# Eight-core attention and quantized-FFN layer: stage barriers replaced by single waits, one LayerNorm loop reordered, attention accumulators reassigned

## What is computed

```
x = hidden_states                        # 16 x 2048 x 1024 f32, two sequences a core
q, k, v = LN(x) @ wq + bq, LN(x) @ wk, LN(x) @ wv + bv   # 16 heads of 64
q, k = rope(q, k)                        # on the last 1024 positions
a = softmax(q k^T / 8) v
x = x + LN(a @ wo + bo)
h = bit_linear(LN(x), w1)                # 1024 -> 4096; activations to 8 bits per token,
h = silu(depthwise_conv1d(h, taps=3))    # weights to -1, 0, 1 times one scale
x = x + LN(bit_linear(h, w2))            # 4096 -> 1024
```

## Time and profile before

| | us |
|---|---|
| median of 11 runs | 4889.68 |
| lowest and highest run | 4879.98, 4936.07 |
| the profiled execution: its time | 4886.25 |
| its span on core 5, the slowest | 4884.7 |
| spans of the eight cores | 4842.8 to 4884.7 |
| busy on core 5: PE, DVE, ACT, POOL | 2952.0, 2054.0, 1861.9, 51.7 |
| mean granted TensorE clock, core 5 | 0.836 |

### The profile page before, as it was taken

The page is one execution under the profiler, slowest core; times in us unless marked ns, Lnnn a source line. Parts: engine busy times, 40 slices in busy tenths (PEclk is TensorE's granted clock), DMA queues, the critical chain, the costliest instruction groups (busy, mean ns, idle before and its releaser), DMA issues. The chain is left out here.

```text
span 4884.7 us, 42219 instructions; the slowest of 8 cores (4842.8 to 4884.7 us)
## 1 busy us (share of the span) xinstructions
PE 2952.0 (60%) x12366; PEld 1063.9 (22%) x12366; DVE 2054.0 (42%) x3536; ACT 1861.9 (38%) x2155; POOL 51.7 (1%) x94
## 2 busy tenths in 40 slices
PE   0000587888884231787888882235885887277677
PEld 0000232211211111331122220112332333133233
DVE  1333332544454444343445545443443444333433
ACT  0113236766772211337677771211221222333322
POOL 0000000000000000000000000000000000100000
PEclk9999998878876665898788886667997998588798
DMA  7776100000000222100000001223111111423231
GB/s 194 259 258 213 52 27 1 3 3 5 3 3 22 67 76 78 37 20 0 3 5 3 3 5 41 67 67 121 50 51 56 48 48 44 142 93 115 87 121 65
DMA packets 154953, 311.69 MB, mean 64 GB/s; under 512 B 65445, under 2 KB 98277, under 8 KB 150630
## 3 DMA queue, kind: packets, MB, share of 16 engines
q1 hardware_dynamic: 139946, 235.54, 14.8%
q0 software_dynamic: 14784, 73.44, 4.5%
HBM read 206.16 MB, written 98.60 MB: 62 GB/s over the span
## 5 line engine op out<-in xcount | busy, mean ns | idle before, releaser
L701 ACT ACTIVATE ptil<-sc,negM 128x1024 bf16<-128x1024 f32 x1024 | 1060.1, 1142 | 389.8 <-PE sc L640 388.9
L637 PE MATMUL sc<-qres,kres 64*128 64x512 bf16 x1024 | 431.7, 422 | 45.6 <-ACT ptil L701 4.5
L640 PE MATMUL sc<-qres,kres 64*128 64x512 bf16 x1024 | 441.7, 432 | 0.0
L711 PE MATMUL accA<-ptil,vres 128*65 128x512 bf16 x768 | 348.8, 454 | 38.2 <-DVE attA L730 37.2
L715 PE MATMUL accA<-ptil,vres 128*65 128x512 bf16 x768 | 320.8, 418 | 75.9 <-DVE attA L730 75.9
L1186 PE MATMUL p2a<-w2q,ring 128*128 128x512 bf16 x1024 | 239.9, 398 | 181.1 <-DVE outt L1203 156.0
L1012 ACT ACTIVATE hsb<-pcA,convb_s 128x512 bf16<-128x512 f32 x128 | 88.2, 689 | 525.8 <-PE pcA L1003 493.4
L875 PE MATMUL pw<-ident,xqtm 128*128 128x128 bf16 x256 | 32.4, 306 | 417.5 <-DVE xqtm L866 417.5
L979 PE MATMUL pwA<-xqd,w1q 128*128 128x512 bf16 x1024 | 245.1, 382 | 44.9 <-DVE hsc L988 44.9
L159 ACT ACTIVATE stat<-stat 128x1 f32<-128x1 f32 x128 | 25.6, 200 | 576.6 <-DVE stat L154 576.6
L979 PE MATMUL pwB<-xqd,w1q 128*128 128x512 bf16 x1024 | 243.3, 381 | 0.0
(11 more groups left out here) (208 smaller groups left out, 4524.5 us busy)
## 6 DMA issues: line engine op xcount, KB each, us to landing
hs_sp<-hsb SPq DMA_DIRECT2D x64, 512.0 KB, 2.6
ring<-hs_sp SPq DMA_DIRECT2D x8, 4096.0 KB, 15.3
wstg<-w1t SPq DMA_DIRECT2D x8, 2048.0 KB, 11.2
wstg<-w1t POOLq DMA_DIRECT2D x8, 2048.0 KB, 13.7
wstg<-w2t SPq DMA_DIRECT2D x8, 2048.0 KB, 11.8
wstg<-w2t POOLq DMA_DIRECT2D x8, 2048.0 KB, 13.1
xra<-x SPq DMA_DIRECT2D x32, 512.0 KB, 3.8
xrb<-x SPq DMA_DIRECT2D x32, 512.0 KB, 4.6
```

What stands on the lines that cost most here:

```text
L637: TE.matmul(sc[sl][:, 0:512], kc_[0:64, kt * 128:(kt + 1) * 128], qc_[0:64, qc * 512:(qc + 1) * 512], start=True, stop=True, tile_position ...
L640: smmv[g] = st.inc(TE.matmul(sc[sl][:, 512:1024], kc_[64:128, kt * 128:(kt + 1) * 128], qc_[64:128, qc * 512:(qc + 1) * 512], start=True, ...
L701: expv[pl] = ss.inc(S.activation(ptil[pl][:], sc[sl][:], AF.Exp, bias=negM[:, p:p + 1], scale=1.0))
L711: TE.matmul(accAd[:], dc4[:, kt, 0:65], ptil[pl][:, 0:512], start=(kt == 0), stop=(kt == NKT - 1))
```

## The change

- All barriers between stages go, except the first one at the start, the one ahead of the w1 stage and the last. In their place stand waits of single engines on the semaphores above, in front of the next stage or inside it.
- In LN1 each tile calls `ln_chain`, which is `ln_stats` and `ln_fin` one after the other; the statistics of the next tile are no longer issued ahead.
- In attention head A alternates between `accA` and `accA2`, and head B always uses `accB`. The A matmul of a block waits for the copies of A two blocks back (`epivA`), the B matmul for the B copy of the block before (`epivB`, the second of the four copies). The order of the four copies stays.

```
-        bar()                                    # weights -> LN1
+        sv.wait(TE); ss.wait(TE); sv.wait(V)
...
-                    ln1_stats(0)
                     for i in range(NT128):
-                        if i + 1 < NT128:
-                            ln1_stats(i + 1)
-                        r_ap, mb_ap, mbv_ = ln_fin((i % 4) * 4, stats_v[i])
+                        dxr[i % 3].wait(V, xload[i])
+                        r_ap, mb_ap, mbv_ = ln_chain(xr[i % 3][:], (i % 4) * 4)
...
-                bar()                            # LN1 -> QKV
+                sv.wait(TE)
+                ss.wait(TE)
...
+                    for qeng in (SY, G):         # ahead of the first load of wsb
+                        dstg[0].wait(qeng)
+                        dstg[1].wait(qeng)
+                        st.wait(qeng)
+                        if s == 0:
+                            dss[0].wait(qeng)
+                            dss[1].wait(qeng)
+                            dsq[0].wait(qeng)
+                            dsq[1].wait(qeng)
+                            sv.wait(qeng)
+                            ss.wait(qeng)
...
-                bar()                            # QKV -> attention
+                    sv.wait(TE)
+                    ss.wait(TE)
...
-                        accAd = accr[(2 * qc) % 3]
-                        accBd = accr[(2 * qc + 1) % 3]
+                        accAd = accA if qc % 2 == 0 else accA2
                         if kt == 0:
-                            sv.wait(TE, epivN[(2 * qc) % 3])
+                            sv.wait(TE, epivA[qc % 2])
                         TE.matmul(accAd[:], ...)
                         if kt == 0:
-                            sv.wait(TE, epivN[(2 * qc + 1) % 3])
+                            sv.wait(TE, epivB)
-                            accBd[:], dc4[:, kt, 65:130], ptil[pl][:, 512:1024],
+                            accB[:], dc4[:, kt, 65:130], ptil[pl][:, 512:1024],
...
+                    dtb[0].wait(TE)
+                    dtb[1].wait(TE)
                     dtb[0].wait(SY)
                     dtb[1].wait(SY)
-                bar()                            # attention -> Wo
+                    sv.wait(TE)
+                    ss.wait(TE)
...
-                bar()                            # Wo -> LN1 of the next sequence
+                st.wait(V)
+                sv.wait(TE)
+                ss.wait(TE)
...
-        bar()                                    # w1 stage -> w2 stage
+            sv.wait(TE)
+            ss.wait(TE)
...
+            drl.wait(G)
+            st.wait(G)
+            dhs.wait(S)
+            dhs.wait(V)
+            dsw.wait(S)
+            dsw.wait(V)
             for c in range(HC):
                 drl.inc(G.dma_start(w2q[:, c * H:(c + 1) * H], w2qt_sp[c]), 16)
...
                     drl.wait(G)
+                    dsw.wait(G)
```

More of the change, by code:

```diff
@@ L348, in build_nc @@
                 s_.wait(SY)
-        bar()
+        sv.wait(TE)
+        ss.wait(TE)
+        sv.wait(V)
         _ph = ExitStack()
@@ L611, in build_nc @@
                     sc = [sc0, sc1]
-                    accr = [accA, accA2, accB]
                     expv = [0, 0, 0]
@@ L615, in build_nc @@
                     epiv = 0
-                    epivN = [0, 0, 0]
+                    epivA = [0, 0]
+                    epivB = 0
                     bcv = 0
@@ L723, in build_nc @@
                             V.tensor_copy(lbufB[0:1, qc * 512:(qc + 1) * 512],
-                                          accBd[64:65, :])
-                            epivN[(2 * qc + 1) % 3] = sv.inc(V.tensor_copy(
+                                          accB[64:65, :])
+                            epivB = sv.inc(V.tensor_copy(
                                 tmpB[p % 2][:, qc * 512:(qc + 1) * 512],
-                                accBd[0:64, :]))
+                                accB[0:64, :]))
                             V.tensor_copy(lbufA[0:1, qc * 512:(qc + 1) * 512],
                                           accAd[64:65, :])
-                            epivN[(2 * qc) % 3] = epiv = sv.inc(V.tensor_copy(
+                            epivA[qc % 2] = epiv = sv.inc(V.tensor_copy(
                                 attA[0:64, p * T + qc * 512:p * T + (qc + 1) * 512],
```

## The result

The change made the kernel faster: ratio 0.959 of the kernel before, 95% interval 0.9557 to 0.9622. On the median of 4889.68 us that is 4689 us, 4673 to 4705 by the interval. The forecast was 4715 us, a ratio of 0.9643, and its range began at 4700, 11 us above what was measured. The direction and the mechanism were right; sizes of single terms were not, the step-36 term and the range's low end above all, and the last part says by how much. The median over all 12 runs is 4703.08 us; four of them had one die at a lower clock, and the ratio leaves such runs out.

What follows compares the result with a forecast made beforehand. ScalarE was taken to set attention's pace where not stopped, mostly by waits for scores; -87.4 - 59.8 - 19.5 - 14.8 + 15.4 - 5.3 = -171.4 from 4886.25 gave 4715 us, range 4700 to 4812.

Steps and rivals of the forecast that it cites:

- the step-36 term: Attention, where the reciprocals are spread: ten waits of 13.16 us take the short form of 11.68, -14.8 us.
- the range's low end: 4700 us: the forecast less 15 for the barriers' far end, LN1's low end and step 36 in its shortest form.
- The LN1 term: LN1 loop: statistics no longer issued ahead expose the square root's round trip, 0.48 us for each of 32 tiles, +15.4 us.
- The border wait: Attention block borders: B's matmul starts earlier, ScalarE's wait falls from 2.04 to 0.63 us at 62 borders, -87.4 us.
- The clock: Attention behind borders: with a TensorE gap of about 0.9 us the clock stays up and 115 slow steps go, -59.8 us.
- the excess of the border waits: Attention borders: waits longer than 2.04 us because their matmuls ran slow lose the excess, -19.5 us.
- Barriers: Between stages: single waits save -5.3 us together, between 0 and -9; -2.9 of it from w2q's earlier load before w2.
- The slowest core: Whole kernel: core 5, last already at the start of attention, stays the slowest.
- No slow spell stayed behind a border: Answers the rival for attention borders that the slow spells all stay: 4809 us, chance 0.10.
- VectorE was not late: Answers the rival that reciprocals hold up B's copy at 28 attention borders: 4993 us, chance 0.04.
- the release that doesn't come: Rival for attention borders: B's matmul still starts only after all four copies, 4896 us, chance 0.06.

Runs made afterwards that it cites:

- the kernel with three copies: Head B's first matmul of a block waits for three copies, not two, against the changed kernel; ratio 0.9788, attention 727.0 and 732.9 us.

## Why the prediction was right, and where it failed

The step that failed is the term for step 36, -14.8 us, together with the low end of the range built on it: measured, the waits at step 36 fell by 24.2 us, and the slow steps behind them, which the sum had at no change, by some 3 more. The LN1 term erred the other way, and the rest of the miss lies in which core is slowest.

- *The border wait.* Right: 1.41 us less at 62 borders; TensorE's gap "about 0.9 us" is 0.93, ScalarE's wait 0.63 is 0.63.
- *The clock.* Right as to whether, and near as to size: the slow steps behind borders cost 57.8 us (forecast 59.8), the excess of the border waits fell by 17.1 (forecast 19.5). The nearest row, QKV's clean gaps of 1.14 us, was the right one to go by, since the new gap of 0.93 us is shorter still. It would not have served for a longer one: at 1.65 us slow steps come, as the kernel with three copies shows. The rule of the Trainium skill (TensorE: Matmul & The Clock Gate, section "A second HAM failure mode: psum-queue depth-cycling") is told without gap lengths; here it holds at 1.65 and 2.35 us and not at 0.93 us, though PSUM buffers are cycled in all three.
- *Step 36: the term that failed in attention.* The prediction put it that step 36 "takes the short form (11.68)", 14.8 us in all. Shorter forms than any row of before had were there. Granted clock in a step 36 of the changed kernel, its first half and then from the fall on:

```profile
887.10:893.40 6.30, 4.27 (x18) 0.92 (x16) 2.05 (x4) 3.22 (x3) 0.00 (x0) 1.00 0.00 1
893.42:903.66 10.24, 7.36 (x18) 1.33 (x18) 5.65 (x8) 2.23 (x2) 0.00 (x0) 0.50 0.00 0
```

  and TensorE's rounds in it:

```profile
891.94 0.61 PE L670 MATMUL pib<-invrA,ones1f 1*64 1x512 f32 x1 [1.65 <-DVE invbB L680]
894.66 1.08 PE L670 MATMUL pib<-invrA,ones1f 1*64 1x512 f32 x1 [1.64 <-DVE invbB L680]
898.27 1.08 PE L670 MATMUL pib<-invrA,ones1f 1*64 1x512 f32 x1 [1.64 <-DVE invbB L680]
```

  The clock falls only after the second round: the rounds are 2.72 us apart at full clock and 3.61 at half. The 14 waits at step 36 sum to 153.9 us, 24.2 less than the 178.1 before and not 14.8, and 37 slow steps follow them (two of 1.81 us among them) instead of 43, another 3 us. The step of the earlier trace rows came right behind a slow spell: the clock was at 0.50 just before it and again from within its second round on, so that its rounds start 2.72, 3.07 and 3.61 us apart, where here they start 2.72, 2.72 and 3.61 apart. It was a row of the disturbed kernel, and I took it for the undisturbed value. That the clock falls at all inside step 36 is not the border's doing: it does so in the changed kernel too, on all eight cores, and not when the pauses are filled.
- *The low end of the range.* It takes 15 us off the forecast for three ends, but the prediction's own figures give 3.7 for the barriers (-9 in place of -5.3), 4.4 for LN1 (+11 in place of +15.4) and about 1 for step 36 at 11.59: some 9 us, a low end of 4706. The 4700 written down missed the measured 4689 as well.
- *LN1: over-sized.* Forecast +15.4, measured about 11 (10.4 inside the loops, 96.2 and 96.8 us to 101.7 twice). The statistics chain of the changed kernel and, behind it, one instruction inside the w2 row:

```profile
529.25 0.68 DVE L146 BATCH_NORM_STATS2 bnbuf<-xra 128x6 f32<-128x512 f32 x1
531.46 0.20 ACT L159 ACTIVATE stat<-stat 128x1 f32<-128x1 f32 x1 [4.36 <-DVE stat L154]
532.20 1.24 ACT L379 ACTIVATE ln1b<-xra,stat 128x1024 bf16<-128x1024 f32 x1 [0.54 <-DVE stat L163]
```

```profile
4367.10 0.15 DVE L151 TENSOR_SCALAR stat<-stat 128x1 f32<-128x1 f32 x1 [0.26 <-DVE stat L149]
```

  The chain is 532.20 - 529.25 = 2.95 us, 0.36 over the 2.59 before. The w2 row had 3.07, 0.12 more: its L151 starts 1.87 us into the chain and not 1.69, which has nothing to do with the square root, and its last hop is 0.06 us shorter.
- *Barriers: the w2 border came as forecast.* The rows that answer to the earlier trace rows, and the last landing in the chain of work:

```profile
3979.17 1.86 PE L1069 MATMUL prow<-identf,s2s 128*1 128x128 f32 x8 [0.93 <-DVE s2row L1073]
3981.57 8.48 POOL L1115 DMA_DIRECT2D w2q<-w2qt_sp  x16 [416.93 <-PE prow L1069]
3983.49 34.84 SPq L1140 DMA_DIRECT2D ring<-hs_sp  x2
```

```profile
3997.96 23.20 DMA w2q<-w2qt_sp
```

  From the last matmul of the row to the load it is 0.54 us on every core and was 3.4 to 3.5, the 2.9 us of the forecast. The load itself takes 39.6 us (3981.57 to 4021.16) where core 5 before had 41.8, but this is the spread between cores and not a gain: the eight cores before lie between 36.5 and 41.8, mean 38.6, those after between 34.4 and 40.6, mean 37.6. `w2q` now leads the ring load by 1.9 us where it trailed by 0.4, and that it gains by this is not shown. The stage is 3.4 us shorter on the mean of the cores.
- *The slowest core.* The prediction subtracted its terms from the slowest core and let core 5 stay the slowest. After the change it is core 3. The mean of the cores fell by 186.6 us, the slowest by 198.9; the stages before the first LN1 tile were 5.5 us shorter in the two cores compared, but in the kernel with only the accumulators changed, whose code there is that of the kernel before, they took 445.3 us, and on the slowest cores of the other runs between 427 and 447. So this is spread between executions and cores, and a range for a whole kernel of this size should leave some 10 us for it each way.
- *Rivals.* No slow spell stayed behind a border, VectorE was not late, and B did start right behind the second copy, while the third ran, which rules out the release that doesn't come.

The sum, for the slowest cores: 12 us too little in attention (9.4 in the waits of step 36, 3 in the slow steps behind it), 5 too much for LN1, and 11 in the weight, w1 and w2 stages, nearly all of it spread between cores and executions; together, with 1 us the other way in Wo and QKV, the 27.5 us between -171.4 and -198.9. On the means over the cores the miss is 15.2 us, of which attention has 10.5.

## What to carry to other kernels

Before pricing a wait by its own length, look at the steps behind it: here 62 waits of 2.4 us on TensorE cost as much again through the clock they took down, and the loop was limited by another engine, which only felt it because TensorE at half clock no longer fitted beside it. Release an accumulator in as few copies as possible and put that copy first; and where a gap can't be closed, matmuls into a free buffer, used by nothing, may buy back the clock. Take the price of an undisturbed state from a row that is itself undisturbed. And read a gain of a few microseconds on all eight cores, since any two of them can differ by as much.

## What the runs showed of the hardware

- Slow steps behind a border against TensorE's gap there: none at 0.93 us, 67 behind 37 of 62 borders at 1.65 us, 160 behind 59 at 2.35 us; none when eight unused matmuls filled most of that last gap.
- In step 36, broadcasts with three pauses of 1.64 us end with the clock at 0.50; with six unused matmuls in each pause it stays at 1.00 and no slow step follows.
- A copy of 65 partitions by 512 from PSUM takes VectorE 0.69 us, as one partition by 512 does (0.69 us), and the same row from SBUF 0.41 us.
